# Composite convolution of level 0 as three half-length products, with the folds and their splits moved

## The reference, cut to what matters

```
out = x
for w, b, mod, typ in (same, upsample, same, downsample):
    s = style @ mod_w.T + mod_b                       # a scale per sample and input channel
    weight = SCALE * w * s[:, None, :, None]
    weight = weight * rsqrt(sum(weight ** 2) + EPS)   # per sample and output channel
    out = conv(out, weight) + b                       # 3 taps; blur after "upsample", before "downsample"
```

## Time and profile before

| what | value |
|---|---|
| median of 3 runs | 991.29 us |
| the profiled execution | 990.33 us, of it span of the trace 988.8 us |
| PE busy | 940.2 us (95%), 4636 instructions |
| PEld busy | 792.4 us (80%) |
| DVE busy | 558.3 us (56%) |
| ACT busy | 376.2 us (38%) |
| POOL busy | 111.0 us (11%) |
| mean granted TensorE clock | 0.978 |

### The profile page before, as it was taken

One profiled execution on the slowest core, in us unless ns is written; L12 is line 12 of the kernel. 1 busy time (PEld: TensorE's weight loads), 2 busy tenths in 40 slices (PEclk: granted clock), 3 DMA queues, 4 the chain that ended last, 5 costly groups with the idle time before them and its releaser, 6 DMA issues.

```text
span 988.8 us, 14065 instructions
## 1 busy us (share of the span) xinstructions
PE 940.2 (95%) x4636; PEld 792.4 (80%) x4636; DVE 558.3 (56%) x1133; ACT 376.2 (38%) x717; POOL 111.0 (11%) x141
## 2 busy tenths in 40 slices
PE   5899999999999999999999998839999999999997
PEld 4777888888888888888888887638888888888886
DVE  8894353353353354344344333966677767777774
ACT  2672243243243243233233221434554445444541
POOL 7100000000000000000000000710112111211121
PEclk8799999999999999999999999859999999999999
DMA  8701011011011011101101101331221222112211
GB/s 281 244 5 65 22 42 64 21 42 64 21 42 64 25 39 64 40 25 63 42 28 57 42 21 54 54 106 29 100 85 64 65 96 94 64 64 87 96 50 64
DMA packets 33567, 64.12 MB, mean 65 GB/s; under 512 B 12304, under 2 KB 13968, under 8 KB 33552
## 3 DMA queue, kind: packets, MB, share of 16 engines
q1 hardware_dynamic: 24480, 30.90, 10.6%
q0 software_dynamic: 9072, 33.03, 9.2%
HBM read 47.14 MB, written 16.78 MB: 65 GB/s over the span
## 4 chain that ended last, share of the span: by engine, by line
PE 88%; DVE 8%; issue 2%; ACT 1%; DMA 1%; POOL 0%; SPq 0%; POOLq 0%; DVEq 0%; ACTq 0%
PE conv_ps L172 9%; PE conv_ps L174 8%; PE conv_ps L173 8%; PE fold_ps L581 6%; PE prod_ps L743 6%; PE prod_ps L744 6%; PE prod_ps L745 6%; PE prod_ps L725 6%; PE prod_ps L726 6%; PE prod_ps L727 6%; PE prod_ps L824 6%; PE prod_ps L823 6%; PE fold_ps L548 3%; PE turn_ps L682 3%; PE turn_ps L704 1%
## 5 line engine op out<-in xcount | busy, mean ns | idle before, releaser
L158 DVE TENSOR_TENSOR h_lo<-conv_ps,h_hi 64x512 fp32r<-64x512 f32 x128 | 88.2, 689 | 47.3 <-ACT h_hi L637 46.4
L172 PE MATMUL conv_ps<-h_hi,e_hi 128*128 128x512 f32 x256 | 104.9, 410 | 2.4 <-issue 2.4
L657 ACT ACTIVATE cond<-conv_ps,bias,demod_tab 128x510 f32<-128x510 f32 x64 | 49.9, 779 | 144.7 <-PE conv_ps L174 132.7
L173 PE MATMUL conv_ps<-h_lo,e_hi 128*128 128x512 f32 x256 | 102.2, 399 | 0.0
L174 PE MATMUL conv_ps<-h_hi,e_lo 128*128 128x512 f32 x256 | 102.1, 399 | 0.0
L743 PE MATMUL prod_ps<-b_hi,xt 128*128 128x512 f32 x256 | 99.9, 390 | 2.3 <-DVE xt L158 2.3
L823 PE MATMUL prod_ps<-quant,xt_hi 128*128 128x512 f32 x256 | 100.3, 392 | 1.4 <-DVE xt_lo L158 1.4
L801 DVE SCALAR_TENSOR_TENSOR res<-prod_ps,norm,res 128x512 f32<-128x512 f32 x32 | 23.9, 750 | 137.3 <-PE prod_ps L745 137.3
L726 PE MATMUL prod_ps<-a_lo,xt 128*128 128x512 f32 x256 | 101.0, 395 | 0.0
L725 PE MATMUL prod_ps<-a_hi,xt 128*128 128x512 f32 x256 | 101.0, 394 | 0.0
L727 PE MATMUL prod_ps<-a_hi,xt 128*128 128x512 f32 x256 | 101.0, 394 | 0.0
(11 more groups left out here) (222 smaller groups left out, 1982.4 us busy)
## 6 DMA issues: line engine op xcount, KB each, us to landing
x_in<-in_x SPq DMA_DIRECT2D x64, 128.0 KB, 2.7
res<-in_x POOLq DMA_DIRECT2D x16, 512.0 KB, 3.6
x_after_first<-res POOLq DMA_DIRECT2D x16, 512.0 KB, 2.9
x_in<-x_after_first SPq DMA_DIRECT2D x64, 128.0 KB, 2.7
res<-x_after_first POOLq DMA_DIRECT2D x16, 512.0 KB, 3.5
out_x<-res POOLq DMA_DIRECT2D x15, 512.0 KB, 2.9
a_raw<-in_adapter_in SPq DMA_DIRECT2D x8, 512.0 KB, 8.1
b_raw<-in_adapter_out SPq DMA_DIRECT2D x8, 512.0 KB, 8.0
```

Source lines behind the costliest of these rows:

```text
L158: return nc.vector.tensor_tensor(out, whole, hi.bitcast(F32), ALU.subtract)
L172: nc.tensor.matmul(out, hi(w), moving_hi(i), start=(i == 0), stop=False)
L173: nc.tensor.matmul(out, hi(w), moving_lo(i), start=False, stop=False)
```

## The change

In level 0 the composite filter is applied in another way. Output columns are taken by parity too, so a row of 512 becomes two of 256. With the four filter tiles e0..e3 and the data at even columns (centre) and odd columns (before, after), two sums of tiles (e0+e1 and e2+e3, the parts 4 and 5 of `whole`) are multiplied with the centre data, and each single tile with a difference of neighbouring data. The result is middle + (conv of differences): `pe_cond` now has 6 stationary tiles x 3 products of 256 columns per sample (18 instead of 12 matmuls, at half the columns). Around it:

- `act_layer1` writes the scaled result into `data` (two operations, even and odd columns); `dve_differences` makes the two rows of differences (2 x 128x257); `act_layer1_hi` and `dve_layer1` split the three rows at once (128x771).
- `act_fold2` copies the filter into `whole` (4 operations), `dve_sum_taps` adds pairs of tiles (128x512), `act_taps` and `dve_taps` split 128x1536.
- The middle goes to `fold_ps[a]`, `act_middle` scales it (128x256), `dve_join` adds it to both halves (128x512) into `cond`; `act_ends` writes the outermost columns in two operations. The gates and score parts share memory with `cond`, `whole` shares it with `v` and `r`, `x_raw` with `x_lo`.
- In `first_step` fold3 goes to the head of the step, fold2 to the place behind the scores, ahead of hidden half 0. `act_fold_start` and `dve_fold_start` of the next pair are done one step earlier.
- Level 1 keeps 4 tiles x 3 products of 512 columns, with the halves swapped so that h needs no shift: `h_hi` and `h_lo` are one operation of 128x512 each. The outputs are shifted by one position.
- In the transition the two `pe_second_cond` of pair 16 stand ahead of all four edge products. All loads of level 1 wait for the last hidden product; a second, rolled copy of the int4 words is loaded.
- SP waits for `layer1_done` ahead of a load of x, since x is loaded where `x_lo` lies. Rows of x in DRAM have two pad words per parity.

Core of the diff:

```
+        def act_layer1(act, c, a, bufs):
+            by_parity = conv_ps[a][:, :].rearrange("p (t two) -> p two t", two=2)
+            for first, parity in ((CENTRE, 0), (ODD + 1, 1)):
+                last = nc.scalar.activation(data[:, first:first + T2], by_parity[:, parity, :], ACT.Identity, bias=..., scale=...)
+            last.then_inc(S.layer1_scaled, 1)
+        def dve_differences(v, c, a, bufs):
+            v.wait_ge(S.layer1_scaled, 2 * c + a + 1)
+            nc.vector.tensor_tensor(data[:, BEFORE:BEFORE + SPAN], data[:, ODD:ODD + SPAN], centre, ALU.subtract)
+            nc.vector.tensor_tensor(data[:, AFTER:AFTER + SPAN], data[:, ODD + 1:ODD + 1 + SPAN], centre, ALU.subtract).then_inc(S.differences, 1)
+        def act_layer1_hi(act, c, a, bufs):
+            act.wait_ge(S.differences, 2 * c + a + 1)
+            nc.scalar.activation(bufs.h_hi[a][:, :], bufs.data[a][:, 0:3 * SPAN], ACT.Identity).then_inc(S.layer1_hi, 1)
+        def pe_cond(pe, c, a, bufs):
+            part(fold_ps[a][:, 0:T2], (5, 4), CENTRE).then_inc(S.middle_done, 1)
+            part(conv_ps[a][:, 0:T2], (3, 1), BEFORE)
+            part(conv_ps[a][:, T2:H], (2, 0), AFTER).then_inc(S.cond_done, 1)
-            products(conv_ps[a][:, :], (3, 2, 1, 0), tiles(bufs.e_hi[:, :, a, :]), ...).then_inc(S.cond_done, 1)
+        def act_taps(act, c, bufs, first=False):
+            act.wait_ge(S.taps_summed, c + 1)
+            nc.scalar.activation(flat(bufs.e_hi[:, :, :, :]), flat(bufs.whole), ACT.Identity).then_inc(S.fold2_hi, 1)
+        def dve_join(v, c, a, bufs):
+            v.wait_ge(S.cond_done, 2 * c + a + 1)
+            v.wait_ge(S.middle_scaled, 2 * c + a + 1)
+            nc.vector.scalar_tensor_tensor(out=out, in0=both, scalar=..., in1=middle, op0=ALU.mult, op1=ALU.add).then_inc(S.joined, 1)
@@ act_fold_start
+                act.wait_ge(S.fold2_ready, c)
@@ first_step of PE
+                pe_fold3(pe, c, buf0)
                 pe_layer1(pe, c, 0, buf0)
                 pe_turn(pe, i, buf0, False)
                 pe_layer1(pe, c, 1, buf0)
-                pe_fold3(pe, c, buf0)
                 pe_scores(pe, i, buf0, first)
+                pe_fold2(pe, c, buf0)
                 pe_hidden(pe, i, 0, buf0, first)
                 pe_score_sum(pe, i, buf0)
-                pe_fold2(pe, c, buf0)
@@ transition of PE
+            for a in range(2):
+                pe_second_cond(pe, NPAIR, a, buf1)
             pe.wait_ge(S.x1_ready, 2 * NPAIR + 1)
-            for layer in range(3):
+            for layer in range(4):
                 edge_tensor(pe, 1, set1, layer)
-            pe_cond(pe, NPAIR, 0, buf1)
-            edge_tensor(pe, 1, set1, 3)
-            pe_cond(pe, NPAIR, 1, buf1)
@@ SP, after hidden_done of pair 15
+            first_loads(sp, 1, set1)
             sp.dma_start(set1.cols[:, :], t["L1_cols"]).then_inc(S.cols_loaded, 16)
```

More of the change, by code:

```diff
@@ L514, in level_buffers, with cond_buffer @@
             b.first_sample = B * L
-            b.x_hi, b.x_lo, b.h_hi, b.h_lo = conv.x_hi, conv.x_lo, conv.h_hi, conv.h_lo
+            b.x_hi, b.x_raw, b.x_lo, b.h_hi, b.h_lo = conv.x_hi, conv.x_raw, conv.x_lo, conv.h_hi, conv.h_lo
             b.v_hi, b.v_lo, b.r_hi, b.r_lo, b.e_hi, b.e_lo = conv.v_hi, conv.v_lo, conv.r_hi, conv.r_lo, conv.e_hi, conv.e_lo
+            b.whole, b.middle, b.data = conv.whole, conv.middle, conv.data
             return b
+        def cond_buffer(T, name, b):
+            b.cond_flat = T(name, [P, 2 * (H + 2)])
+            b.cond = b.cond_flat[:, :].rearrange("p (a h) -> p a h", a=2)
         def act_fold_start(act, c, bufs, first=False):
@@ L596, in act_fold2 @@
[L596 to L606 removed]
+            act.nop(nofuse=True)
@@ L632, in act_layer1 @@
             act.nop(nofuse=True)
-            ps, hi = conv_ps[a], bufs.h_hi[a]
+            data = bufs.data[a]
+            by_parity = conv_ps[a][:, :].rearrange("p (t two) -> p two t", two=2)
+            for first, parity in ((CENTRE, 0), (ODD + 1, 1)):
+                last = nc.scalar.activation(data[:, first:first + T2], by_parity[:, parity, :], ACT.Identity, bias=at(bias1, c, a, bufs),
+                                            scale=at(scale1, c, a, bufs))
+            last.then_inc(S.layer1_scaled, 1)
@@ new lines, in dve_layer1 @@
+        def dve_layer1(v, c, a, bufs):
+            v.wait_ge(S.layer1_hi, 2 * c + a + 1)
+            low(bufs.h_lo[a][:, :], bufs.data[a][:, 0:3 * SPAN], bufs.h_hi[a][:, :]).then_inc(S.layer1_ready, 1)
+        def pe_cond(pe, c, a, bufs):
+            if a == 0:
+                pe.wait_ge(S.fold2_ready, c + 1)
+            pe.wait_ge(S.layer1_ready, 2 * c + a + 1)
+            cut = lambda w, first: (lambda u: w[a][:, first + u:first + u + T2])
+            part = lambda out, filters, data: products(out, filters, tiles(bufs.e_hi[:, :, a, :]), tiles(bufs.e_lo[:, :, a, :]),
+                                                       cut(bufs.h_hi, data), cut(bufs.h_lo, data))
+            part(fold_ps[a][:, 0:T2], (5, 4), CENTRE).then_inc(S.middle_done, 1)
+            part(conv_ps[a][:, 0:T2], (3, 1), BEFORE)
+            part(conv_ps[a][:, T2:H], (2, 0), AFTER).then_inc(S.cond_done, 1)
@@ new lines, in act_middle @@
+        def act_middle(act, c, a, bufs):
+            act.wait_ge(S.middle_done, 2 * c + a + 1)
+            act.nop(nofuse=True)
+            nc.scalar.activation(bufs.middle[a], fold_ps[a][:, 0:T2], ACT.Identity, bias=at(bias4, c, a, bufs),
+                                 scale=at(demod_tab[:, LAYERS - 1, :], c, a, bufs)).then_inc(S.middle_scaled, 1)
+        def dve_join(v, c, a, bufs):
+            v.wait_ge(S.cond_done, 2 * c + a + 1)
+            v.wait_ge(S.middle_scaled, 2 * c + a + 1)
+            v.nop(nofuse=True)
+            out = bufs.cond[:, a, 1:H + 1].rearrange("p (t two) -> p two t", two=2)
+            both = conv_ps[a][:, :].rearrange("p (two t) -> p two t", two=2)
+            middle = bufs.middle[a].unsqueeze(1).broadcast_to([P, 2, T2])
+            nc.vector.scalar_tensor_tensor(out=out, in0=both, scalar=at(demod_tab[:, LAYERS - 1, :], c, a, bufs), in1=middle,
+                                           op0=ALU.mult, op1=ALU.add).then_inc(S.joined, 1)
@@ new lines, in act_ends @@
+        def act_ends(act, c, a, bufs):
+            act.wait_ge(S.joined, 2 * c + a + 1)
+            n = 2 * c + a - bufs.first_sample
+            ends = cond_edge[:, :, n:n + 1] if isinstance(n, int) else cond_edge[:, :, bass.ds(n, 1)]
+            ends = ends.rearrange("p s u -> p (s u)")
+            nc.scalar.activation(bufs.cond[0:C, a, 1::-1], ends[0:C, :], ACT.Identity)
+            nc.scalar.activation(bufs.cond[C:P, a, 0:H:H - 1], ends[C:P, :], ACT.Identity).then_inc(S.cond_ready, 1)
@@ L1152, in edge_tiles, with middles, ends @@
                 tile_hi(L, s, "down")
-            def ready(L):
+            def middles(L, c, bufs):
                 act.wait_ge(S.bias4_ready, L + 1)
+                for a in range(2):
+                    act_middle(act, c, a, bufs)
+            def ends(L, c, bufs):
                 act.wait_ge(S.edges_done, L + 1)
+                for a in range(2):
+                    act_ends(act, c, a, bufs)
             nc.scalar.preload_act_table(ACT.Sqrt)
```

325 lines of the change are left out of this document (199 added, 126 removed).

## The result

The changed kernel takes 1008.17 us (median of 4 runs, 1007.83 to 1009.73), the kernel before 991.08 us (4 runs, 990.24 to 991.54): ratio 1.0177, 95% interval 1.0159 to 1.0194. It is slower; the forecast was 991.5 us, and the range ended at 999.

The account below looks back on a forecast made before the run. PE's own list was taken to bound the steps, DVE's list the head and step 0. On 990.33 us, +15.4 - 13.4 - 2.0 + 0.2 = +0.2; with 0.96 to the median 991.5 us, range 984 to 999.

Parts of the forecast that it names:

- the main term: Cond in steps 1 to 14: 18 half-length products at 0.118 us, 4.44 instead of 5.66 us, 1.22 us less a step.
- weight loads: Rival for the half-length products: each needs its load's 192 ns, 1.25 us lost a step, 1028 us in all; chance 3%.
- The scores' wait: Steps 1 to 14: without fold3 ahead of them, the scores wait 0.34 us for the transposed pair's split, paid in full.
- Steps 1 to 14: Steps of level 0: 1.3 us of PE removed, 0.34 of wait added; 0.96 us gained a step, 13.4 in all.
- 0.1 us for fold2: Steps 1 to 14: fold2, now behind the scores, saves its slow start once, about 0.1 us a step.
- Head and step 0: Start of the kernel: DVE's longer list delays cond, fold3 and adapter out; step 1 starts at 102.1, 15.4 us lost.
- the high end of the range: Head and step 0: half clock after PE's wait before adapter out adds 1.7, to 17.1; longer `data` operations 2 more, 19.
- Transition: Between the levels: two conds fill PE's wait ahead of the edge products; 2 us gained, ends 1.5 lost to 4 gained.
- signs of being wrong: Fold2 period over 36.2 or under 35.3; step 1 starting before 98 or after 106; a transition that grows.
- Level 1's steps keep their PE list: 0.: Steps of level 1: PE's list is unchanged, so they keep their old pace; 0 us.
- Tail: End of the kernel: one more small operation of ACT before the last transposes; 0.2 us lost.
- the head decides for slower: Rival, head and step 0: DVE's list and the lower clock cost 17.1 to 19 us, about 995.2 us in all; chance 28%.

Follow-up runs that it names:

- fold3_mid: Changed kernel with fold3 moved between the transposes and layer1 of sample 1, ahead of the scores: 1003.57 us, ratio 1.0103.
- same_addresses: Changed kernel with padding alone, giving v, r, quant, xt_hi and xt_lo of level 1 the kernel before's addresses modulo 2048 bytes: 1003.18 us, one run.
- vlo_first: Changed kernel with v_hi and v_lo of step 0 ahead of two roundings on ACT and four splits of A on DVE: 1004.35 us, ratio 1.0102.
- kept_busy: Changed kernel with extra products that nobody reads in PE's waits in step 0, pair 15 and tail: 1005.51 us, ratio 1.0124.
- old_transition: Changed kernel with both conds of pair 16 back inside the edge chain, behind the third and fourth edge products: 1004.22 us, one run.
- changed_again: Changed kernel without any edit, run again: 1007.13 us, ratio 1.0156.
- before_moved: Kernel before, with padding that gives v, r, quant and xt of level 1 the changed kernel's addresses modulo 2048 bytes: 996.37 us, one run.

## Why the prediction was wrong

**What held.** The bound, and the main term: 18 half-length products at 0.12 us, cond 4.39 us against 4.44 forecast; weight loads don't bound them. The scores' wait was 0.33 us against 0.34, and fold3_mid shows that it was paid in full. Nothing else in the step waits. By the list of what overlaps in the Trainium skill ("TensorE: Matmul & The Clock Gate", section "The mechanism") loads overlap only with products on other rows of the array (the paragraph above that list also allows for a background weight buffer). With loads of 0.19 us and products 0.12 us apart these rows disagree with the list, as fold2's did.

**Steps 1 to 14, a size.** 0.72 us a step, not 0.96. The forecast booked 0.1 us for fold2, which no longer stands behind the score sum. It is saved there (1.78 against 1.88), but hidden half 1 took its place and pays it (5.70 against 5.59), and the scores, now behind a wait, pay another 0.10 (1.05 against 0.95). The first product behind the small sum is slow whoever stands there. Another 0.04 is in adapter out (10.91 against 10.87) and 0.02 in hidden half 0 (5.60 against 5.58), and cond gives 0.05 more than forecast. same_addresses gives 0.05 us a step back, but nearly all of it in fold2 (1.74 instead of 1.78), so what adapter out and hidden half 0 lost stays open. 14 x 0.24 = 3.3 us.

**Head and step 0, a size.** The mechanism was as told (vlo_first, fold3_mid); the place erred by 2.7 us. Cond began 1.0 us later than forecast, and by fold3 it was 1.9 us, since DVE waits 1.40 and 1.84 us for PE's edge product and second cond, the former at the lower clock in part. Adapter out, for which the trace's 10.87 us were taken, took 12.33 behind its wait. The granted clock of 0.61 in its first 3.6 us, and 1.00 with 11.06 us in kept_busy, show that this is the clock: it had been counted at the high end of the range, not in the value.

**Transition, the failed step.** The forecast said: two conds fill the wait, and the 4 us of cond inside the chain are gone and "the chain finds PE warm", 2 us gained. The later start was right (664.99 - 641.01 against 652.12 - 631.27, 3.1 us later against pair 16's layer1). That the chain would be shorter without the cond was wrong. From the first edge product to the end of the first layer1 of level 1 it takes 688.41 - 664.99 = 23.42 us, and with both conds in it, in the kernel before, it took 675.71 - 652.12 = 23.59. Both conds worked there. The first covered the last edge split of DVE (1.53 us of wait now). The fourth edge product took 1.92 us behind it, at a granted clock of 1.00, and takes 4.02 now at 0.50. The second covered DVE's split of the next x (1.88 us of wait now), and the layer1 behind it took 1.39 us and takes 2.72 at the lower clock. These four make 6.8 us, as much as the two conds had taken there (4.06 and 2.90). Warm was PE only for the first edge product: the granted clock is 1.00 from 665 to 667 and 0.50 from 669 to 689, behind DVE's 4.3 us. These waits and durations stand in all nine traces of this order, so the mechanism is shown; its size differs from execution to execution (see old_transition). Of the forecast's own signs of being wrong this one came: the transition grew.

A further 1.65 us is adapter half 0 of pair 15 at the lower clock (7.27 against 5.62). That is chance of the two executions compared and not the change: changed_again has 5.66 and before_moved 7.06.

**Level 1, a term that was missing.** "Level 1's steps keep their PE list: 0." The list stayed and the pitch (the time from start to start) didn't: 20.09 against 19.91 us a step, 14 x 0.19 = 2.6 us by the addresses, shown by same_addresses and before_moved. The first layer1 adds the 1.33 us named above.

**Tail.** 0.44 us for ACT's additional small operations (PE waits 1.10 instead of 0.67 us for them; forecast 0.2), and 1.60 us of quant half 0 at the lower clock (5.38 against 3.78), which kept_busy takes back. The kernel before has the same wait of 1.41 us ahead of it and stays at 1.00; why the clock falls in one and not in the other stays open.

The rival "the head decides for slower" decided from a step 1 behind 104.1, and it was 104.73; its 995.2 us was still 13 us short, as it too had the transition as a gain and level 1 at 0. Of the 17.3 us that the forecast missed between these two executions, 6.0 are the lower clock at four places (step 0 1.46, pair 15 1.65, the first layer1 of level 1 1.33, tail 1.60), 3.6 the transition, 3.3 the steps, 2.6 addresses, 1.2 the head; 0.6 are in small ones.

## What to carry to other kernels

An operation that stands in a chain of small dependent steps can hide the other engines' work there and hold TensorE's clock up: before it is moved, list what it covers in its old place. Price the stretch behind every new wait at the lower clock too. And when buffers are added, compare the pitch of unchanged products before any other theory: their addresses may have moved. Before a stretch of one trace is put down to a change, look for the same stretch in the traces that don't have the change.
